# DVE order around the second projection of an attention step: one rotation ahead of a block transpose, token sums inverted ahead of both

## The chip, the cores and the metric

The kernel runs on one core of one Trainium2 chip. The metric is the device time in microseconds (us) of one execution, as the median of the runs shown. Three runs of the kernel before gave 1044.98, 1046.76 and 1047.56 us. Five engines work side by side, each on its own queue of instructions in program order, and wait for each other only through semaphores: PE (TensorE: matmuls and transposes), DVE (VectorE), ACT (ScalarE), POOL (GpSimd) and SP, which issues the DMAs here.

## The reference, cut to what matters

The input is 64 sequences of 256 rows by 192 columns. Three layers follow each other:

```
# 1: token layer: 16 tokens become 8, by attention over the tokens
q = einsum('bndt,st->bnds', xv, Wq) + bq ; kv = einsum('bndt,st->bnds', xv, Wkv) + kv_bias
attn = softmax(einsum('bnds,bndr->bnsr', q * scale, k)) ; h = q' + einsum('bnsr,bndr->bnsd', attn, v)
# 2: attention over the 128 rows of a sequence, 12 query heads, 3 key and value heads of 64, rotary embedding
q, k = apply_rope(q, cos, sin), apply_rope(k, cos, sin)      # q, k, v = layernorm(h) @ Wq, Wk, Wv
h = h + softmax(q k^T * SCALE) v @ Wo
# 3: feed-forward layer, 192 -> 768 -> 192
h = h + gelu(layernorm(h) @ W_in + b_in) @ W_out
```

## The kernel before, in words

A step p handles two sequences, a = 0 and a = 1, and the three layers are staggered: the attention of pair p runs beside the token layer of pair p + 1 and the feed-forward layer of pair p - 1. The host-side function `run` writes `step` out for p = -1, 0 and 1, puts p = 2 to 30 in a loop of 29 passes, and writes out p = 31, 32 and 33. Every engine has its own `step`; the order of its work is the order of the code, written by hand.

What belongs to the attention of one sequence, and who does it: PE projects (`qkv`, three banks of the ring of that sequence, `RING[a]`); DVE multiplies each bank by the cosine and by the sine table (`rotate`, lines L491 and L493, outputs `rot_c` and `rot_s`); POOL adds the two products of banks 0 and 1 to `q_tok` (L396, one addition for a bank, 384 columns), DVE adds those of the keys to `k_tok` (`keys_added`, L501 and L504); PE turns the six tiles of `q_tok` and the two of `k_tok` (`qk_turned`, L690), ACT copies them to `qkT` (L296), and PE multiplies them to scores (L711). DVE takes the maxima (`key_max`, L515), ACT the exponentials with their sums (`score_exp`, L302), DVE inverts the sums (`sums_inverted`, L535), POOL multiplies (`probs`, L404), and DVE turns the probabilities in blocks of 32 by 32 into `EB` (`blocks_turned`, L526, a `STREAM_TRANSPOSE` for each of three groups k = 0, 1, 2). SP then moves `EB` through DRAM to `ET` so that whole rows are turned (`blocks_moved`): groups 0 and 1 make the first piece, group 2 the second. Each piece is one write (`spill`, L231) and four reads (L237). PE multiplies `ET` with the values (`probs_v`, L728).

The token layer's softmax has ACT's exponentials `t_e` with the sums `t_sum` (L340), DVE's inverse `t_rs` (L597 before, L595 after), ACT's scaling `t_a` (L344), and PE's transposes of `t_a` (L803).

The change lies on DVE only, where the second sequence's projection comes in while the first sequence's probabilities are still to be turned. SP's queue holds, in this order: first piece written, second piece written, four reads of the first, four reads of the second, and then the store of the result. In the loop the counts that semaphores are waited for depend on p, so the queue also holds register instructions between the engine's own.

Of the kernel before, what the change touches and what calls it, by code (L numbers as in the profile page):

```python
# [82 lines left out]
def program(nc, x, w_tok, b_tok, bq_row, w_att1, w_att2, wo, w_in1, w_in2, b_in, w_out,  # L83
# [4 lines left out]
    with ExitStack() as ctx:  # L88
# [102 lines left out]
        def need(eng, s, value):  # L191

            if not isinstance(value, int) or value > 0:
                eng.wait_ge(s, value)
# [239 lines left out]
        def _(dve):  # L434
# [41 lines left out]
            def step(p, att, tok, ffn, fin):  # L476
                n = p + 1

                def rotate(a, banks):

                    if banks[0] == 0:
                        need(dve, q_out, 4 * (p - 1) + 2 * a + 2)
                    for b in banks:
                        heads = 6 if b < 2 else NKV
                        src = RING[a][:, 512 * b:512 * b + heads * HD]
                        c = slice(b * BANKW, b * BANKW + heads * HD)
                        dve.wait_ge(qkv_mm, 6 * p + 3 * a + b + 1)
                        cos_t, sin_t = (rope_qc, rope_qs) if b < 2 else (rope_c, rope_s)
                        cos = cos_t[:].rearrange("p (o d) -> p o d", o=1).broadcast_to([P, heads, HD])
                        sin = sin_t[:].rearrange("p (o t d) -> p o t d", o=1, t=2).broadcast_to([P, heads, 2, HALF])  # L490
                        nc.vector.tensor_tensor(rot_c[:, a, c].rearrange("p (h d) -> p h d", d=HD),  # L491
                                                src.rearrange("p (h d) -> p h d", d=HD), cos, ALU.mult)
                        nc.vector.tensor_tensor(rot_s[:, a, c].rearrange("p (h t d) -> p h t d", t=2, d=HALF),  # L493
                                                src.rearrange("p (h t d) -> p h t d", t=2, d=HALF)[:, :, ::-1, :],
                                                sin, ALU.mult).then_inc(rot_out, 1)

                def keys_added(a):
                    need(dve, qT_mm, 4 * (p - 1) + 2 * a + 2)
                    dve.wait_ge(rot_out, 6 * p + 3 * a + 3)
                    c = slice(DQ, DQ + 2 * HD)  # L500
                    nc.vector.tensor_tensor(k_tok[:, a, 0:2 * HD], rot_c[:, a, c], rot_s[:, a, c], ALU.add)  # L501
                    c = slice(DQ + 2 * HD, DQ + DKV)
                    kc, ks = (r[:, a, c].rearrange("p (o d) -> p o d", o=1).broadcast_to([P, 2, HD]) for r in (rot_c, rot_s))
                    nc.vector.tensor_tensor(k_tok[:, a, 2 * HD:].rearrange("p (o d) -> p o d", o=2),  # L504
                                            kc, ks, ALU.add).then_inc(k_out, 1)
# [14 lines left out]
                def blocks_turned(a, k, q):  # L520
                    g = GROUPS[k]
                    s0, heads = PIECES[g // 2]
                    h0 = REP * g - s0
                    dve.wait_ge(prob_out, 6 * q + 3 * a + k + 1)
                    need(dve, spilled[g // 2], 16 * (2 * (q - 1) + a + 1))
                    nc.vector.transpose(  # L526
                        EB[:, a, s0 * P:(s0 + heads) * P].rearrange("p (j h c) -> p h j c", j=NB, h=heads)[:, h0:h0 + REP],
                        E[:, a, 512 * g:512 * (g + 1)].rearrange("p (h j r) -> p h j r", h=REP, j=NB)
                    ).then_inc(blocks_out, 1)
# [11 lines left out]
                def attention_stats(a, done):  # L541
                    dve.wait_ge(h2_out, done)
                    stats(h2, st2, mv2, a, ln2_st, ln2_mv, done)
# [46 lines left out]
                    sums_inverted(0, 2, p)  # L590
                if ffn:
                    attention_stats(1, 2 * p)
                if att:
                    blocks_turned(0, 1, p)
                if tok:  # L595
                    dve.wait_ge(t_exp, 2 * n + 2)
                    nc.vector.reciprocal(t_rs[:], t_sum[:]).then_inc(t_rcp, 1)  # L597
                if att:
                    rotate(1, (0, 1))
                    blocks_turned(0, 2, p)  # L600
                    rotate(1, (2,))
                    keys_added(1)
# [47 lines left out]
                if att:  # L650
# [4 lines left out]
                    attention_stats(0, 2 * p + 1)  # L655

            run(dve, step)

        @block.tensor
# [280 lines left out]
```

## Time and profile before

| | |
|---|---|
| median of three runs | 1046.76 us |
| profiled execution, its own time | 1043.57 us |
| its span | 1041.7 us |
| granted TensorE clock, mean | 0.986 |
| PE busy | 988.7 us, 95% of the span |
| DVE busy | 810.2 us, 78% |
| ACT busy | 730.3 us, 70% |
| POOL busy | 434.3 us, 42% |
| mean traffic of the DMA engines | 122 GB/s |

Engine names in the views: PE is the matmul side of TensorE and PEld its weight loads, which run ahead of the matmuls; SPq is SP's queue of DMA issues; DVEq are the instructions that DVE's sequencer handles alone (register operations, waits, branches) and that aren't counted as busy. A row of a timeline begins with the start from the begin of the span and the duration, both in us; at its end stands in brackets how long the engine had been idle before it, and what ended that.

### The profile page before, as it was taken

The page shows a single profiled execution, that of the slowest core. Times are in us where ns is not written, and L with a number is a line of the kernel's source. Part 1 is how long each engine was busy: PE and PEld are TensorE (multiplying, and loading weights), DVE is VectorE, ACT ScalarE, POOL GpSimd, SP SyncE. Part 2 cuts the span into 40 slices and gives each one's busy share as a digit, 9 for nine tenths or more (in the row PEclk, how much of TensorE's full clock was granted, in tenths as well). Part 3 has the DMA queues.
Part 4 walks back from the last instruction along what each step waited for, and adds up shares of the span by engine and source line. Part 5 has one row for each costly group of instructions (what it writes and reads, how often), then busy time and mean ns, then how long its engine had stood idle before and what let it go on. Part 6 is the DMA issues. An engine that isn't in the chain of part 4 may idle for free. (4 is left out here: it accounts for less than half of the span.)

```text
span 1041.7 us, 24501 instructions
## 1 busy us (share of the span) xinstructions
PE 988.7 (95%) x7232; PEld 856.5 (82%) x7232; DVE 810.2 (78%) x2095; ACT 730.3 (70%) x2531; POOL 434.3 (42%) x583
## 2 busy tenths in 40 slices
PE   3689999999999999999999999999999999999986
PEld 2567888888988888888888888888888888888875
DVE  2678888778878878888877888887788887788861
ACT  2456776787776677677677777667867767777761
POOL 0334444444544443454444444435345444434440
PEclk8789999999999999999999999999999999999999
DMA  5134434334434434443433454443444344344331
GB/s 176 43 110 132 140 103 143 120 109 128 149 119 118 139 110 119 138 141 109 135 124 105 128 149 123 113 141 110 121 134 144 113 128 128 108 121 149 109 119 46
DMA packets 139935, 127.49 MB, mean 122 GB/s; under 512 B 30992, under 2 KB 123024, under 8 KB 139920
## 3 DMA queue, kind: packets, MB, share of 16 engines
q1 hardware_dynamic: 137632, 124.16, 39.9%
q10 hardware_dynamic: 2288, 3.15, 0.9%
q8 instruction: 7, 0.11, 0.0%
q14 instruction: 8, 0.07, 0.0%
HBM read 70.63 MB, written 56.62 MB: 122 GB/s over the span
## 5 line engine op out<-in xcount | busy, mean ns | idle before, releaser
L404 POOL TENSOR_TENSOR E<-E,e_rcp 128x512 f32<-128x512 f32 x192 | 198.4, 1040 | 282.4 <-DVE e_rcp L535 279.3
L302 ACT ACTIVATE E<-ring,m_neg 128x128 f32<-128x128 f32 x768 | 271.4, 388 | 55.5 <-DVE m_neg L515 55.4
L396 POOL TENSOR_TENSOR q_tok<-rot_c,rot_s 128x384 f32<-128x384 f32 x128 | 125.4, 1000 | 127.8 <-DVE rot_s L493 127.8
L302 ACT ACTIVATION_READ_ACCUMULATOR E<-ring,m_neg 128x1 f32 x768 | 174.8, 228 | 0.0
L515 DVE TENSOR_REDUCE m_neg<-ring 128x4 f32<-128x512 f32 x192 | 122.5, 680 | 54.1 <-PE ring L711 54.1
L296 ACT COPY qkT<-ring 128x512 f32<-128x512 f32 x128 | 71.9, 587 | 127.0 <-PE ring L690 127.0
L526 DVE STREAM_TRANSPOSE EB<-E 128x512 f32<-128x512 f32 x192 | 133.9, 698 | 17.7 <-POOL E L404 17.7
L842 PE MATMUL ring<-wo_sb,OT 128*128 128x192 f32 x768 | 141.6, 335 | 1.7 <-ACT OT L310 1.7
L698 PE MATMUL bank<-wout_sb,G 128*128 128x192 f32 x768 | 135.4, 326 | 2.9 <-ACT G L370 2.9
L842 PEld LDWEIGHTS ring<-wo_sb,OT 128*128 128x128 f32 x768 | 124.3, 191 | 5.0 <-issue 2.6
L698 PEld LDWEIGHTS bank<-wout_sb,G 128*128 128x128 f32 x768 | 125.4, 190 | 3.5 <-ACT G L370 3.4
L711 PEld LDWEIGHTS ring<-qkT 64*128 64x128 f32 x1536 | 90.7, 187 | 29.8 <-ACT qkT L296 29.8
L711 PE MATMUL ring<-qkT 64*128 64x128 f32 x1536 | 103.0, 280 | 5.0 <-ACT qkT L296 1.4
L728 PE MATMUL ring<-ET,v_tok 128*64 128x512 f32 (+1 forms) x512 | 96.8, 499 | 1.1 <-DMA ET<-spill 1.1
L491 DVE TENSOR_TENSOR rot_c<-ring,rope_qc 128x384 f32<-128x384 f32 x128 | 69.8, 545 | 14.9 <-issue 12.2
L664 PE MATMUL ring<-WH,XH 128*128 128x384 f32 x192 | 73.8, 384 | 1.5 <-DVE XL L647 1.5
L493 DVE TENSOR_TENSOR rot_s<-ring,rope_qs 128x384 f32<-128x384 f32 x128 | 69.8, 545 | 0.0
L728 PEld LDWEIGHTS ring<-ET,v_tok 128*64 128x64 f32 x512 | 31.0, 136 | 46.1 <-issue 35.7
L690 PE MATMUL ring<-ident,q_tok 128*128 128x128 f32 x384 | 60.4, 280 | 7.5 <-POOL q_tok L396 7.4
L664 PE MATMUL ring<-W2S,XL 128*128 128x384 f32 x192 | 65.2, 340 | 0.0
L664 PE MATMUL ring<-WL,XH 128*128 128x384 f32 x192 | 65.2, 340 | 0.0
L664 PE MATMUL ring<-WH,XL 128*128 128x384 f32 x192 | 65.1, 339 | 0.0
(125 smaller groups left out, 2258.6 us busy)
## 6 DMA issues: line engine op xcount, KB each, us to landing
spill<-EB SPq DMA_DIRECT2D x64, 512.0 KB, 2.7
ET<-spill SPq DMA_DIRECT2D x256, 128.0 KB, 2.8
spill<-EB SPq DMA_DIRECT2D x64, 256.0 KB, 2.1
ET<-spill SPq DMA_DIRECT2D x256, 64.0 KB, 2.3
x_sb<-in_x_dram SPq DMA_DIRECT2D x64, 192.0 KB, 2.5
out_dram<-out_sb SPq DMA_DIRECT2D x64, 96.0 KB, 2.3
x_sb<-in_x_dram SPq DMA_DIRECT2D x64, 64.0 KB, 2.3
w_raw<-in_w_att_dram ACTq DMA_DIRECT2D x2, 576.0 KB, 4.8
```

Of the source, the lines that this page charges most:

```text
L296: nc.scalar.copy(qkT[:, a, c], RING[a][:, c]).then_inc(qT_out, 1)
L302: last = nc.scalar.activation(E[:, a, s * P:(s + 1) * P], RING[a][:, s * P:(s + 1) * P], ACT.Exp, bias=m_neg[:, a, s:s + 1], accum_out=e_s ...
L396: nc.gpsimd.tensor_tensor(q_tok[:, a, c], rot_c[:, a, c], rot_s[:, a, c], ALU.add).then_inc(q_out, 1)
L404: nc.gpsimd.tensor_tensor(e, e, r, ALU.mult).then_inc(prob_out, 1)
L491: nc.vector.tensor_tensor(rot_c[:, a, c].rearrange("p (h d) -> p h d", d=HD), src.rearrange("p (h d) -> p h d", d=HD), cos, ALU.mult)
L515: nc.vector.tensor_reduce(m_neg[:, a, REP * g:REP * (g + 1)], RING[a][:, 512 * g:512 * (g + 1)].rearrange("p (h k) -> p h k", k=P), AX_X, ...
L526: nc.vector.transpose(EB[:, a, s0 * P:(s0 + heads) * P].rearrange("p (j h c) -> p h j c", j=NB, h=heads)[:, h0:h0 + REP], E[:, a, 512 * g: ...
L664: last = nc.tensor.matmul(out_ap, lhsT, rhs, start=(i == 0), stop=(i == len(terms) - 1))
L698: last = nc.tensor.matmul(B6[:, a * D:(a + 1) * D], G[:, m, a * P:(a + 1) * P], wout_sb[:, m, :], start=(m == 0), stop=(m == NM - 1))
L711: last = nc.tensor.matmul(RING[a][:, s * P:(s + 1) * P], qkT[rows, a, t * P:(t + 1) * P], qkT[rows, a, k0:k0 + P], start=True, stop=True)
L728: last = nc.tensor.matmul(RING[a][k * HD:(k + 1) * HD, 512 * b:512 * b + n_cols], v_tok[:, a, g * HD:(g + 1) * HD], src.rearrange("p i h c ...
L842: last = nc.tensor.matmul(ATT_Y, OT[:, a, t * P:(t + 1) * P], wo_sb[:, t, :], start=(t == 0), stop=(t == 5))
```

## The change

It moves two instructions of DVE in every step with attention: the inverse of the token sums (with its wait) goes ahead of the block transpose of group 1 of the first sequence, and so does the rotation of bank 0 of the second sequence. The block transpose now stands between the rotations of bank 0 and bank 1. No instruction is added or removed, and the four other engines keep their queues.

```
-                if att:
-                    blocks_turned(0, 1, p)
                 if tok:
                     dve.wait_ge(t_exp, 2 * n + 2)
                     nc.vector.reciprocal(t_rs[:], t_sum[:]).then_inc(t_rcp, 1)
                 if att:
-                    rotate(1, (0, 1))
+                    rotate(1, (0,))
+                    blocks_turned(0, 1, p)
+                    rotate(1, (1,))
                     blocks_turned(0, 2, p)
                     rotate(1, (2,))
                     keys_added(1)
```

On DVE, in the body of the loop, behind the statistics of the first layer norm input `h` (BN_STATS and BN_AGGR); the instructions named ISA and REGISTER_ALU are the sequencer's own, which work out the count to wait for:

```order
 L465 BN_STATS st<-h 128x6 [waits h2_out]
 L467 BN_AGGR mv<-st 128x2 [waits ln2_st]
-L526 STREAM_TRANSPOSE EB<-E 128x4x4x32 [waits spilled_01,prob_out]
-L596 ISA
-L597 RECIPROCAL t_rs<-t_sum 128x2 [waits t_exp]
+L594 ISA
+L595 RECIPROCAL t_rs<-t_sum 128x2 [waits t_exp]
 L194 REGISTER_ALU
 L487 REGISTER_ALU [waits q_out]
 L491 TENSOR_TENSOR rot_c<-ring,rope_qc 128x384 [waits qkv_mm]
 L493 TENSOR_TENSOR rot_s<-ring,rope_qs 128x384
+L526 STREAM_TRANSPOSE EB<-E 128x4x4x32 [waits spilled_01,prob_out]
```

The transpose has moved down past a register instruction, the inverse, two more register instructions and the rotation of bank 0; what stood directly behind the aggregate is now the inverse with its wait for ACT.

On DVE in the last step with attention, p = 31, which has no token layer and no register instructions:

```order
 L467 BN_AGGR mv<-st 128x2 [waits ln2_st]
-L526 STREAM_TRANSPOSE EB<-E 128x4x4x32 [waits spilled_01,prob_out]
-L491 TENSOR_TENSOR rot_c<-ring,rope_qc 128x384 [waits qkv_mm,q_out]
-L493 TENSOR_TENSOR rot_s<-ring,rope_qs 128x384
+L491 TENSOR_TENSOR rot_c<-ring,rope_qc 128x384 [waits qkv_mm,q_out]
+L493 TENSOR_TENSOR rot_s<-ring,rope_qs 128x384
+L526 STREAM_TRANSPOSE EB<-E 128x4x4x32 [waits spilled_01,prob_out]
```

Here only the transpose and the rotation of bank 0 have changed places.

## Rows read from the trace of the kernel before

**Rows 1.** The view by windows, one pass of the loop; busy us of each engine.

```profile
core 0: us, PE busy (x) PEld busy (x) DVE busy (x) ACT busy (x) POOL busy (x), PEclk, DMA share, GB/s
500.00:530.73 30.73, 30.43 (x228) 26.53 (x227) 25.10 (x67) 22.77 (x79) 13.56 (x18) 1.00 0.42 126
```

**Rows 2.** The view of waits, whole span: us in total, times, longest.

```profile
POOL q_tok L396 <- DVE rot_s L493: 127.8, 65, 6.5
...
PEld ring L690 <- POOL q_tok L396: 16.0, 35, 1.1
...
DVE rot_c L491 <- issue: 12.2, 29, 0.5
```

**Rows 3.** The timeline of DVE in one pass of the loop.

```profile
509.19 0.18 DVE L535 RECIPROCAL e_rcp<-e_sum 128x4 f32<-128x4 f32 x1 [0.44 <-ACT E L302]
...
509.77 0.18 DVE L467 BATCH_NORM_AGGREGATE mv<-st 128x2 f32<-128x6 f32 x1 [0.16 <-DVE st L465]
509.88 0.71 DVE L526 STREAM_TRANSPOSE EB<-E 128x512 f32<-128x512 f32 x1
510.51 0.12 DVE L597 RECIPROCAL t_rs<-t_sum 128x2 f32<-128x2 f32 x1
510.55 0.53 DVE L491 TENSOR_TENSOR rot_c<-ring,rope_qc 128x384 f32<-128x384 f32 x1
511.01 0.55 DVE L493 TENSOR_TENSOR rot_s<-ring,rope_qs 128x384 f32<-128x384 f32 x1
...
511.94 0.54 DVE L493 TENSOR_TENSOR rot_s<-ring,rope_qs 128x384 f32<-128x384 f32 x1
...
514.11 0.28 DVE L504 TENSOR_TENSOR k_tok<-rot_c,rot_s 128x128 f32<-128x128 f32 x1
```

**Rows 4.** The timeline of POOL, same pass.

```profile
510.76 0.57 POOL L388 TENSOR_TENSOR rs<-ve,half_neg 128x1 f32<-128x1 f32 x1
511.63 1.96 POOL L396 TENSOR_TENSOR q_tok<-rot_c,rot_s 128x384 f32<-128x384 f32 x2 [0.31 <-DVE rot_s L493]
```

**Rows 5.** The timeline of PE's weight loads, same pass.

```profile
513.64 0.31 PEld L690 LDWEIGHTS ring<-ident,q_tok 128*128 128x128 f32 x3 [0.41 <-POOL q_tok L396]
...
514.52 0.30 PEld L690 LDWEIGHTS ring<-ident,k_tok 128*128 128x128 f32 x2
...
515.74 1.42 PEld L711 LDWEIGHTS ring<-qkT 64*128 64x128 f32 x24 [0.36 <-ACT qkT L296]
```

**Rows 6.** The timeline of ACT, same pass.

```profile
508.87 0.29 ACT L302 ACTIVATION_READ_ACCUMULATOR E<-ring,m_neg 128x1 f32 x1
...
509.64 0.28 ACT L340 ACTIVATION_READ_ACCUMULATOR t_e<-t_s,t_neg 128x1 f32 x1
510.67 0.70 ACT L344 ACTIVATE t_a<-t_e,t_rs 128x128 f32<-128x128 f32 x2 [0.74 <-DVE t_rs L597]
```

**Rows 7.** The timeline of DVE where one pass of the loop ends.

```profile
525.84 0.18 DVE L467 BATCH_NORM_AGGREGATE mv<-st 128x2 f32<-128x6 f32 x1 [0.16 <-DVE st L465]
526.45 0.56 DVE L491 TENSOR_TENSOR rot_c<-ring,rope_qc 128x384 f32<-128x384 f32 x1 [0.43 <-issue]
```

**Rows 8.** DVE's sequencer, lines L596, L194, L487: duration ns, first and last start.

```profile
L596 DVEq FUSED_REGOPS  x1: 64/64/64, 509.9 to 509.9; - x1
```

```profile
L194 DVEq ALU_OP  x1: 40/40/40, 510.0 to 510.0; - x1
```

```profile
L487 DVEq ALU_OP  x5: 40/40/40, 510.1 to 526.7; - x5
```

**Rows 9.** The timelines of SP's queue and PE's loads; the page's DMA issues.

```profile
510.70 0.35 SPq L231 DMA_DIRECT2D spill<-EB  x1
...
513.70 3.67 SPq L237 DMA_DIRECT2D ET<-spill  x8
...
521.26 0.14 PEld L728 LDWEIGHTS ring<-ET,v_tok 128*64 128x64 f32 x2 [0.29 <-issue]
...
ET<-spill SPq DMA_DIRECT2D x256, 64.0 KB, 2.3
```

More of the change, by code:

```diff
@@ L592, in step @@
                     attention_stats(1, 2 * p)
-                if att:
-                    blocks_turned(0, 1, p)
                 if tok:
@@ L598, in step @@
                 if att:
-                    rotate(1, (0, 1))
+                    rotate(1, (0,))
+                    blocks_turned(0, 1, p)
+                    rotate(1, (1,))
                     blocks_turned(0, 2, p)
```

## The prediction, written before the run

> **What bounds the kernel now.** I read the windows first. One pass of the loop takes 30.73 us, PE is busy for 30.43 of it, DVE for 25.10 and POOL for 13.56 [rows 1]. So a pass is as long as PE's queue with the few short waits in it, and the change, which leaves PE's queue alone, can act only through one of those waits. The view of waits names the one that the moved instructions lead to: PE's weight loads stand for 16.0 us in total, 35 times, before the transposes L690, until POOL has added `q_tok`; POOL in turn waits for DVE's `rot_s` [rows 2]. The loop has 29 passes, so this is a wait of every pass.
>
> Then the timelines of one pass, engine by engine, to see which of the two banks ends that wait. DVE rotates bank 0 from 510.55, with `rot_s` from 511.01 to 511.56; `rot_s` of bank 1 ends at 511.94 + 0.54 = 512.48 [rows 3]. POOL starts its two additions at 511.63, which is 0.07 behind the first `rot_s`, and is through at 511.63 + 1.96 = 513.59 [rows 4]. PE's load for the second three tiles comes at 513.64, 0.05 later, after 0.41 idle [rows 5]. So PE waits for bank 1 of `q_tok`, not for bank 0: the load before the first three tiles shows no wait. What follows on PE, the two tiles of keys at 514.52 and the scores at 515.74, which wait for ACT's copy of the turned tiles, hangs on the same chain [rows 5].
>
> When does POOL's second addition start? The two take 1.96 together, so half of that behind 511.63, at 512.61. What it needs from DVE is there at 512.48 + 0.07 = 512.55. POOL is the later one by only 0.06 us. That is the slack of the whole path; the rest of the argument is on which side of it the change lands.
>
> **What the change does, part by part.**
>
> *The transpose goes behind the rotation of bank 0.* It occupies DVE's queue for 510.51 - 509.88 = 0.63 us [rows 3]. With the inverse directly behind the aggregate, and nothing lost between, the inverse would start at 509.88 and the rotation at 510.55 - 0.63 = 509.92. Its `rot_s` would end 0.63 earlier, at 510.93. POOL can't use all of this: its `rs` runs until 510.76 + 0.57 = 511.33 [rows 4], so its first addition could start 0.30 earlier. But bank 1 is still behind the same transpose: the sum of work in front of its `rot_s` is what it was. So 512.48 stays at best, POOL's second addition can start at 512.55 at best, and the gain on PE is at most 0.06 us a pass, 29 x 0.06 = 1.7 us. Ahead of it stands the key path too: `k_tok` is done at 514.11 + 0.28 = 514.39 and isn't moved earlier, and PE starts on it at 514.52 [rows 3, 5]; with the 0.05 of a handoff to PE that is 0.08 of room, so no larger gain could pass there either.
>
> *The inverse goes in front, with its wait for ACT.* In the row order of before it stands at 510.51, when ACT has long been done. Now it's due at 509.88. ACT's second sum of `t_e` is read out at 509.64 + 0.28 = 509.92 [rows 6]. How long such a handoff takes is seen one row above: the sum of the last score exponential ends at 508.87 + 0.29 = 509.16, and DVE's inverse starts at 509.19, 0.03 later [rows 3, 6]. So the inverse starts at 509.95, and DVE has lost 0.07 us. Behind the waiting instruction is all of DVE's queue: both rotations, both transposes, the keys. That ACT's `t_a`, now at 510.67 after 0.74 idle, comes some 0.5 us earlier [rows 6] is worth nothing: PE turns `t_a` only behind the feed-forward matmuls, and that load shows no wait.
>
> *The register instructions lose their cover.* Between the inverse and `rot_c` the loop has two register instructions of the sequencer, and the second has a wait. Before, the sequencer ran through them at 510.0 and 510.1, while the engine was still in the transpose of 0.71 us, and the row of `rot_c` at 510.55 shows no idle time [rows 3, 8]. Now the engine's only work in front of them is the inverse, which takes the queue for 0.04 us (510.51 to 510.55). They show up as idle time of DVE. How much: the register instructions on L596, L194 and L487 start at 509.9, 510.0 and 510.1, so about 0.1 apart though their own durations are 0.064 and 0.040 [rows 8]. Two of them, less the 0.04 that the inverse covers, give 0.16 us. The trace has one place where this is bare: at the end of a pass the aggregate starts at 525.84 and `rot_c` at 526.45, after 0.43 us in which DVE waited for nothing but issue, and this happens 29 times, once for each pass [rows 2, 7]. There four sequencer instructions, with a branch among them, stand between. Compared with the 0.11 from an aggregate to its follower (509.77 to 509.88), they cost 0.61 - 0.11 = 0.50, or 0.13 each, which puts two of them at 0.25. From below the bound is nothing at all, if the sequencer still gets through while aggregate and inverse run. I take 0.16, the nearer row since it is of these very instructions without a branch; the ends 0 and 0.25 go to the range.
>
> The Trainium skill speaks on both sides here, and neither figure enters the sum. "Advanced Engine Details and Errata", Sequencer Loop, says that other engine instructions can be read and queued while a control instruction executes; read broadly, the register instructions stay hidden and the change costs 0.07 instead of 0.23 a pass. "Vector Engine (DVE) Microarchitecture Reference", section 1.2, says that a semaphore wait is issued before the opcode is even read and that every DVE instruction takes the full dispatch; by that nothing behind the inverse is read before ACT is done, and both register instructions are bare. The row of the loop's end, with 0.43 us of issue, sides with the second.
>
> *Sum for a pass.* DVE from the rotation of bank 1 on is later by 0.07 + 0.16 = 0.23 us. Its `rot_s` then ends at 512.71, POOL starts on it at 512.78 instead of 512.61, and PE's load moves from 513.64 to 513.81: 0.23 - 0.06 = 0.17 us. The keys, at 514.39 + 0.23 + 0.05 = 514.67, are just in time for PE at 514.52 + 0.17 = 514.69. DVE's later work of the pass (the normalised `hn` directly behind the keys, the maxima of the scores) is late by 0.23 rather than 0.17, and PE's transposes of `hn` follow those; so for PE the pass gets longer by 0.17 to 0.23, and I take 0.20. Nothing further down gives it back, as all that PE waits for in a pass is itself started by PE's results. 29 passes give 5.8 us.
>
> *The steps outside the loop.* They have no register instructions. Step 1 pays the wait of about 0.07; steps 0 and 31 nothing that I can price above 0.1. Together 0.1 us.
>
> *The DMAs.* The first piece is complete one transpose later. It moves from 509.88 to behind `rot_s` of bank 0: 0.23 late plus two rotations of 0.46, so the write issued at 510.70 goes out at about 511.85 [rows 3, 9]. The reads, from 513.70 for 3.67 us, shift by the same 1.15: the eighth is issued by 518.5. It needs 2.3 us to land: 520.8. PE loads for the second piece at 521.26 at the earliest, and 0.2 later with the change [rows 9]. That leaves over 0.4 us, so I cost it at nothing; it is the thinnest cover in this sum. SP's write of the second piece, its store of the result and the next pass's writes wait for DVE and PE anyway.
>
> In all 5.9 us. The profiled execution took 1043.57 us (its span of 1041.7 and 1.9 around it) and would take 1049.5. It lies 3.2 us below the median of the runs, 1046.76, and I put the same difference on the median: 1052.7 us.
>
> **The rivals.**
>
> *Hidden register instructions.* DVE loses only the 0.07 of the wait, the slack of 0.06 on POOL takes nearly all, and the pass grows by 0.01 to 0.07: 0.3 to 2 us, so 1047 to 1048.8. For it: the sequencer is seen ahead of its engine by half a microsecond in rows 8 against rows 3. Against it: it can't be ahead right behind a wait that it has just sat through, and 0.43 us of bare issue in every pass. This is the case in which the kernel isn't slower; it decides if `rot_c` starts before about 510.05 on the scale of these rows.
>
> *Gain.* The full 0.06 a pass from POOL's earlier first addition, which needs a wait and a dispatch that both cost nothing: 1.7 us, 1045.1. Even this is inside what a measurement can tell. A gain beyond 3 us needs a path that I haven't seen.
>
> *Absorbed.* DVE loses 0.23 us and PE its 0.2 at the transposes, but a later wait of PE in the pass is set by something that hasn't moved. PE's idle time in a pass is 30.73 - 30.43 = 0.30 in all [rows 1], so there is little to absorb it in; most could be a half, 2.9 us, 1049.6.
>
> *Late reads.* If the read of the second piece lands in 3 us or more instead of 2.3, PE waits at L728 for up to 0.3 us more in a pass, on top of the forecast: 8.7 us more, 1061.
>
> **How the numbers follow.** A change of 0.3%, 3.1 us, is about what a measurement of this kernel can tell from none. The forecast has a chance of 0.66, with its own range from 1050 (0.11 a pass) to 1055.2 (0.07 + 0.25 - 0.03 = 0.29 a pass, 8.4 us). The hidden case has 0.17, the absorbed one 0.08, late reads 0.05, a gain 0.04. Slower by over 0.3%: 0.66 + 0.05 and a third of the absorbed case, 0.73. Faster: of the gain and of what I haven't seen, 0.05. Within: 0.22. The range that is to hold 8 in 10 reaches from the hidden case to the upper end of the register cost: 1046.7 to 1055.6.
>
> **What would show it.** In a pass of the changed kernel: the inverse directly behind the aggregate, 0.15 to 0.2 behind its start, with a small wait for ACT; `rot_c` of bank 0 with 0.1 to 0.3 us idle before it that is put down to issue, 29 times; POOL's first addition right behind its `rs` and its second with idle time before it, where it had none; PE's wait at the second L690 at about 0.6 instead of 0.41; a pass of about 30.93 us. I am wrong if `rot_c` follows the inverse within 0.05 us, if the pass stays at 30.73, or if PE's loads L728 show a wait for DMA.

## The result, and the profile after

The changed kernel takes 1051.84 us in the median (1050.87 to 1052.5) against 1045.88 us for the kernel before on the same chip (1044.98 to 1047.56). The ratio is 1.0054, with a 95% interval from 1.0041 to 1.0067: slower by 4.3 to 7.0 us. The forecast was 5.9 us.

The first look is at the length of a pass, by the starts of the token inverse on DVE, twenty passes apart, in the timeline of DVE of the changed kernel:

```profile
203.71 0.17 DVE L595 RECIPROCAL t_rs<-t_sum 128x2 f32<-128x2 f32 x1
...
822.23 0.17 DVE L595 RECIPROCAL t_rs<-t_sum 128x2 f32<-128x2 f32 x1
```

(822.23 - 203.71) / 20 = 30.93 us, against 30.73 before [rows 1]. 29 passes of 0.20 us more are 5.7 us, which is the measured difference; what the few steps outside the loop add can't be told apart.

The same stretch of DVE as in [rows 3] shows where in the pass it is lost:

```profile
512.79 0.18 DVE L467 BATCH_NORM_AGGREGATE mv<-st 128x2 f32<-128x6 f32 x1 [0.16 <-DVE st L465]
512.97 0.17 DVE L595 RECIPROCAL t_rs<-t_sum 128x2 f32<-128x2 f32 x1
513.15 0.56 DVE L491 TENSOR_TENSOR rot_c<-ring,rope_qc 128x384 f32<-128x384 f32 x1
513.63 0.55 DVE L493 TENSOR_TENSOR rot_s<-ring,rope_qs 128x384 f32<-128x384 f32 x1
514.09 0.70 DVE L526 STREAM_TRANSPOSE EB<-E 128x512 f32<-128x512 f32 x1
514.72 0.52 DVE L491 TENSOR_TENSOR rot_c<-ring,rope_qc 128x384 f32<-128x384 f32 x1
515.16 0.54 DVE L493 TENSOR_TENSOR rot_s<-ring,rope_qs 128x384 f32<-128x384 f32 x1
```

Count from the aggregate. Before, `rot_s` of bank 1, the last thing that POOL needs, started 511.94 - 509.77 = 2.17 us behind it; now it is 515.16 - 512.79 = 2.37. `rot_c` of bank 1, in front of it, started at 1.70 in the kernel before (the row below, left out between two of [rows 3]) and starts at 1.93 now: DVE has lost 0.23 us there, for the same instructions.

```profile
511.47 0.55 DVE L491 TENSOR_TENSOR rot_c<-ring,rope_qc 128x384 f32<-128x384 f32 x1
```

The inverse starts 0.18 behind the aggregate, where the transpose stood at 0.11, and `rot_c` follows the inverse after 0.18 instead of 0.04. The 0.18 in front of the inverse is the wait for ACT, whose second sum of the changed kernel's pass is read out at 512.67 + 0.27 = 512.94, 0.03 before the inverse starts:

```profile
512.67 0.27 ACT L340 ACTIVATION_READ_ACCUMULATOR t_e<-t_s,t_neg 128x1 f32 x1
```

The register instruction L594 also stands in front of the inverse, but it isn't what sets this time: in step 1, which is written out and has no such instruction, the inverse follows the aggregate after 0.18 as well (79.68 and 79.86 in DVE's timeline, with ACT's sum read out by 79.84).

POOL shows what the change gave and what it took, in its timeline of the changed kernel, to be set against [rows 4]:

```profile
513.77 0.57 POOL L388 TENSOR_TENSOR rs<-ve,half_neg 128x1 f32<-128x1 f32 x1
514.31 1.00 POOL L396 TENSOR_TENSOR q_tok<-rot_c,rot_s 128x384 f32<-128x384 f32 x1
515.78 1.00 POOL L396 TENSOR_TENSOR q_tok<-rot_c,rot_s 128x384 f32<-128x384 f32 x1 [0.47 <-DVE rot_s L493]
```

The first addition now follows `rs` directly, 0.3 us earlier than before. The second stands still for 0.47 us until the rotation behind the transpose is through. PE needs the second, and its weight loads wait for it 0.60 instead of 0.41 us [rows 5]:

```profile
516.83 0.31 PEld L690 LDWEIGHTS ring<-ident,q_tok 128*128 128x128 f32 x3 [0.60 <-POOL q_tok L396]
```

Over the whole span that wait has gone from 16.0 to 22.4 us [rows 2], which is 0.2 us a pass:

```profile
PEld ring L690 <- POOL q_tok L396: 22.4, 35, 1.2
...
PEld ring L728 <- DMA ET<-spill: 3.0, 4, 1.2
```

The second line is the thin cover of the prediction. The kernel before had nearly the same wait for the reads, so the later write of the first piece costs nothing here:

```profile
PEld ring L728 <- DMA ET<-spill: 2.5, 3, 1.4
```

In the changed kernel SP's queue issues the write 514.91 - 512.79 = 2.12 us behind the aggregate, before it was 510.70 - 509.77 = 0.93 [rows 3, 9]:

```profile
514.91 1.79 SPq L231 DMA_DIRECT2D spill<-EB  x2
```

### The profile page after: what moved, and what is told of

It is laid out like the page before. It is cut to its first block and busy times, and to the rows that moved or that the text cites. A ratio compares the mean times of both kernels' runs of the same rounds, so it can differ in the third digit from the quotient of the medians.

```text
span 1049.1 us, 24501 instructions
## 1 busy us (share of the span) xinstructions
PE 990.7 (94%) x7232; PEld 858.0 (82%) x7232; DVE 815.1 (78%) x2095; ACT 731.5 (70%) x2531; POOL 434.5 (41%) x583
## 5 line engine op out<-in xcount | busy, mean ns | idle before, releaser
L664 PE MATMUL ring<-W2S,XH 128*128 128x384 f32 x192 | 65.2, 339 | 0.0
```

Source lines behind the costliest of these rows:

```text
L664: last = nc.tensor.matmul(out_ap, lhsT, rhs, start=(i == 0), stop=(i == len(terms) - 1))
```

## The experiments

The time of a pass is, as above, from the starts of the inverse twenty passes apart; ratios are against the kernel before on the same chip. "To bank 1" is the time from the aggregate to `rot_c` of bank 1 on DVE, in a pass in the middle of the span, and good to 0.01 us, as the rows are rounded. The experiments are called e1 to e3, r2, b0 to b2 and d1, as in the table.

| kernel | to bank 1, us | pass, us | ratio (95% interval) |
|---|---|---|---|
| before | 1.70 | 30.73 | 1 |
| changed | 1.93 | 30.93 | 1.0054 (1.0041 to 1.0067) |
| e1, inverse only | 1.80 | 30.83 | 1.0029 (1.0017 to 1.0041) |
| e2, rotation only | 1.81 | 30.80 | 1.0016 (1.0005 to 1.0028) |
| e3, counts ahead | 1.82 | 30.79 | 1.0028 (1.0015 to 1.0040) |
| r2, two more counts | 2.12 | 31.12 | 1.0109 (1.0093 to 1.0124) |
| b0, plain, both banks ahead | 1.31 | 30.69 | 0.9979 (0.9970 to 0.9988) |
| b1, counts and both banks ahead | 1.08 | 30.45 | 0.9909 (0.9895 to 0.9923) |
| b2, second transpose later | 1.07 | 30.53 | 0.9934 (0.9920 to 0.9947) |
| d1, POOL's copy ahead | 1.71 | 30.87 | 1.0017 (1.0007 to 1.0026) |

**The inverse alone.**

```
+                if tok:
+                    dve.wait_ge(t_exp, 2 * n + 2)
+                    nc.vector.reciprocal(t_rs[:], t_sum[:]).then_inc(t_rcp, 1)
                 if att:
                     blocks_turned(0, 1, p)
-                if tok:
-                    dve.wait_ge(t_exp, 2 * n + 2)
-                    nc.vector.reciprocal(t_rs[:], t_sum[:]).then_inc(t_rcp, 1)
-                if att:
                     rotate(1, (0, 1))
```

> Only the inverse of the token sums goes ahead; the transpose follows it directly and both rotations stay behind the transpose, with their register instructions. Theory A (my sum: two separate losses on DVE, the wait for ACT and the uncovered register instructions): the inverse starts 0.18 behind the aggregate, the transpose about 0.08 behind that, DVE is late by 0.11 to 0.15 instead of 0.23, and less the 0.06 of POOL's slack the pass takes 30.78 to 30.82 us instead of 30.73: 1.5 to 2.6 us slower than before. Theory B (all of the loss is the inverse in front with its wait): DVE late by 0.23, pass 30.93, 5.6 us slower. Theory C (it is the transpose behind the rotation and the late first write): no loss, 0 us.

```profile
542.42 0.18 DVE L467 BATCH_NORM_AGGREGATE mv<-st 128x2 f32<-128x6 f32 x1 [0.16 <-DVE st L465]
542.59 0.17 DVE L595 RECIPROCAL t_rs<-t_sum 128x2 f32<-128x2 f32 x1
542.68 0.71 DVE L526 STREAM_TRANSPOSE EB<-E 128x512 f32<-128x512 f32 x1
543.31 0.52 DVE L491 TENSOR_TENSOR rot_c<-ring,rope_qc 128x384 f32<-128x384 f32 x1
```

In the timeline of DVE of e1 the inverse starts 0.17 behind the aggregate, and the transpose 0.09 behind the inverse. With the transpose as cover, `rot_c` follows it after 0.63, as in the kernel before. The loss is 0.10 us on DVE and 0.10 in the pass: half of the change's, so theory B (all of it is the inverse) and theory C (none of it) both fall. It is a little more than theory A's upper end in the pass (30.82) and in the kernel (3.0 us slower, 1.8 to 4.3, against 2.6), since nothing of POOL's slack of 0.06 took it up. The expectation had overlooked why: here bank 0 is late as well, so POOL's two additions start later as one piece and end 546.33 - 542.42 = 3.91 behind the aggregate, against 513.59 - 509.77 = 3.82 before [rows 3, 4].

```profile
544.37 1.96 POOL L396 TENSOR_TENSOR q_tok<-rot_c,rot_s 128x384 f32<-128x384 f32 x2 [0.41 <-DVE rot_s L493]
```

**The rotation alone.**

```
                 if att:
+                    rotate(1, (0,))
                     blocks_turned(0, 1, p)
...
                 if att:
-                    rotate(1, (0, 1))
+                    rotate(1, (1,))
```

> Only the rotation of bank 0 goes ahead of the transpose; the inverse stays behind the transpose, in front of the rotation of bank 1. Theory A: no wait for ACT, but two register instructions bare behind the aggregate: rot_c 0.20 to 0.26 behind the aggregate instead of the 0.11 of a covered follower, DVE late by 0.1 to 0.15, pass 30.77 to 30.82, 1.2 to 2.6 us slower than before. Theory B (all of it is the inverse): 0 us or up to 1.7 us faster. Theory C (late first write): the same as the change, 5.6 us slower.

```profile
542.84 0.18 DVE L467 BATCH_NORM_AGGREGATE mv<-st 128x2 f32<-128x6 f32 x1 [0.16 <-DVE st L465]
543.04 0.56 DVE L491 TENSOR_TENSOR rot_c<-ring,rope_qc 128x384 f32<-128x384 f32 x1
```

Here only the two register instructions stand between the aggregate and `rot_c`, and no wait for ACT: 0.20 us from start to start in DVE's timeline of e2, against 0.11 for the transpose in the kernel before. DVE loses 0.11 by bank 1, the pass 0.07. Theory A holds. POOL's first addition is early here, so the slack counts: the second ends 546.72 - 542.84 = 3.88 behind the aggregate, 0.06 later than before for a DVE that is 0.11 late.

```profile
545.72 1.00 POOL L396 TENSOR_TENSOR q_tok<-rot_c,rot_s 128x384 f32<-128x384 f32 x1 [0.36 <-DVE rot_s L493]
```

In this kernel the write of the first piece comes nearly as late as in the change (the transpose starts 1.14 us behind the aggregate, there 1.30), and the kernel loses a third of it, so theory C falls again.

**The counts ahead.** The order of the change, with the counts of the first rotation and its waits put between BN_STATS and BN_AGGR (in the file by a function that is handed to `stats`, for the second sequence only; shown here where it takes effect).

```
                 nc.vector.bn_stats(st[:, a, :], src[:, a, :]).then_inc(s_st, 1)
+                need(dve, q_out, 4 * (p - 1) + 4)
+                dve.wait_ge(qkv_mm, 6 * p + 4)
```

> The order of the change, but the counts and waits of the rotation of bank 0 are worked out between the two statistics instructions, where the engine waits anyway, so no register instruction stands between inverse and rotation. Theory A: inverse to rot_c 0.08 us instead of 0.18, DVE late by 0.13, pass 30.80 to 30.83, 3 us faster than the change and about 2 to 2.5 slower than before. Theory B and theory C: no difference from the change, 5.6 us slower than before.

```profile
540.92 0.18 DVE L469 BATCH_NORM_AGGREGATE mv<-st 128x2 f32<-128x6 f32 x1
541.12 0.17 DVE L602 RECIPROCAL t_rs<-t_sum 128x2 f32<-128x2 f32 x1
541.20 0.54 DVE L498 TENSOR_TENSOR rot_c<-ring,rope_qc 128x384 f32<-128x384 f32 x1
```

From inverse to `rot_c` it is now 0.08 us, where the change has 0.18: the register instructions cost 0.10 together. The pass is 0.14 shorter than that of the change. The ratio of the whole kernel is less sharp (1.0028, 1.6 to 4.2 us slower than before), but its interval ends just below where the change's begins.

**Two more of them.** Dose against effect: two further waits in front of the changed kernel's rotation, for counts long reached, which bring two more register instructions.

```
                 if att:
+                    need(dve, q_out, 4 * p - 5)
+                    need(dve, q_out, 4 * p - 3)
                     rotate(1, (0,))
```

> The changed kernel with two more register instructions of the sequencer (two further waits on the same semaphore for lower counts, long reached) between the inverse and the rotation of bank 0. Theory A (bare register instructions cost about 0.085 to 0.1 us each on DVE and nearly as much in the pass): inverse to rot_c 0.35 to 0.38 us instead of 0.18, pass 31.07 to 31.12 us instead of 30.92, 10 to 11.5 us slower than before. Theory B (they are hidden or it is the pipeline's own restart): pass 30.92, 5.7 us slower than before like the change.

```profile
547.61 0.17 DVE L595 RECIPROCAL t_rs<-t_sum 128x2 f32<-128x2 f32 x1
547.99 0.56 DVE L491 TENSOR_TENSOR rot_c<-ring,rope_qc 128x384 f32<-128x384 f32 x1 [0.21 <-PE ring L666]
```

0.38 us from inverse to `rot_c`, 0.20 more than in the change, and the pass grows by 0.19 to 31.12 us: about 0.1 us for each such instruction, on DVE and in the pass alike. The kernel is 11.4 us slower than before. The idle time has a label that misleads. The last matmul of that bank, in PE's timeline below, is through at 546.88, 1.1 us before `rot_c`; what DVE waited for was its own sequencer.

```profile
546.54 0.34 PE L666 MATMUL ring<-W2S,XL 128*128 128x384 f32 x1
```

**Both banks ahead.** The same parts as the change, with the transpose behind both rotations instead of between them.

```
                 if att:
-                    rotate(1, (0,))
-                    blocks_turned(0, 1, p)
-                    rotate(1, (1,))
+                    rotate(1, (0, 1))
+                    blocks_turned(0, 1, p)
                     blocks_turned(0, 2, p)
```

> The change with one thing different: the block transpose goes behind the rotations of both banks instead of between them; the inverse with its wait stays in front and the register instructions stay bare. Theory A: DVE loses its 0.23 us but rot_s of bank 1 is no longer behind the transpose, so POOL's second addition follows the first at once and q_tok is complete 0.25 us earlier than before, POOL's copy lets the keys through earlier, and what then sets PE is hn on DVE, about as late as before or 0.05 later: pass 30.68 to 30.78, 1.5 us faster to 1.5 slower than before, in any case 4 us or more faster than the change. Rival (the keys' own work on DVE sets PE, late by 0.23): pass 30.85 to 30.93, 3.5 to 5.8 us slower than before.

```profile
539.89 1.96 POOL L396 TENSOR_TENSOR q_tok<-rot_c,rot_s 128x384 f32<-128x384 f32 x2
541.80 0.49 POOL L418 COPY h_cur<-h_next 128x384 f32<-128x384 f32 x1
```

```profile
543.05 0.20 PEld L689 LDWEIGHTS ring<-ident,k_tok 128*128 128x128 f32 x2 [0.23 <-DVE k_tok L504]
543.57 0.42 PEld L827 LDWEIGHTS bank<-ident,hn 128*128 128x128 f32 x4 [0.32 <-DVE hn L473]
```

POOL's two additions run without a gap (first fence), and PE no longer waits for `q_tok` in the loop; it waits 0.23 us for the keys and 0.32 for `hn` instead (second fence, PE's weight loads). The kernel is 2.2 us faster than the one before (1.3 to 3.1), a little more than expected, of which 29 passes of 0.04 us are 1.3. DVE carries the same two losses as in the change. So what denied the change its gain is that the second bank stayed behind the transpose.

**Both banks and the counts ahead.** As b0, with the counts ahead as in e3, and with the inverse between the two rotations instead of in front of them.

> Counts ahead as in e3_counts_ahead; then the rotation of bank 0, the inverse, the rotation of bank 1, and only then the two transposes and the keys. Theory A: rot_c 0.10 behind the aggregate, nothing lost; POOL's first addition follows its rs at once and its second follows without idle time, so q_tok is done 0.25 to 0.3 us earlier; but the keys are where they were, with 0.08 of room, and hn with less: pass 30.65 to 30.73, 0 to 2.3 us faster than before. Theory C (late first write): the first piece is complete 1.5 us later than before, PE waits at L728 and the kernel is over 5 us slower.

```profile
535.13 0.18 DVE L469 BATCH_NORM_AGGREGATE mv<-st 128x2 f32<-128x6 f32 x1
535.23 0.52 DVE L498 TENSOR_TENSOR rot_c<-ring,rope_qc 128x384 f32<-128x384 f32 x1
...
536.13 0.15 DVE L604 RECIPROCAL t_rs<-t_sum 128x2 f32<-128x2 f32 x1
536.21 0.54 DVE L498 TENSOR_TENSOR rot_c<-ring,rope_qc 128x384 f32<-128x384 f32 x1
...
539.03 0.29 DVE L508 TENSOR_TENSOR k_tok<-rot_c,rot_s 128x128 f32<-128x128 f32 x1
539.24 0.28 DVE L511 TENSOR_TENSOR k_tok<-rot_c,rot_s 128x128 f32<-128x128 f32 x1
```

`rot_c` comes 0.10 behind the aggregate, so neither loss is left. The kernel takes 1035.40 us in the median against 1045.08, a ratio of 0.9909: 9.5 us less by the ratio, of which 29 passes of 0.28 us are 8.1. That is far more than the 2.3 us of theory A's upper end, and theory C falls. The size of the gain was the surprise, and the last two rows have a reason: the first keys addition takes 0.29 us here and the second follows after 0.21. In the change, and in the kernel before it, the first took 0.45 to 0.47 and the second followed after 0.36 to 0.40. The keys are done 539.52 - 535.13 = 4.39 us behind the aggregate, before it was 514.39 - 509.77 = 4.62 [rows 3].

**What holds the keys.** In the kernel before, POOL's copy of `h_next` to `h_cur`, which follows the second `q_tok` addition, is put ahead of POOL's `rs`.

```
+                if att:
+                    wait_apart(pool, pool_passed, (h2_out, 2 * p))
+                    nc.gpsimd.tensor_copy(h_cur[:], h_next[:]).then_inc(h_kept, 1)
                 if ffn:
                     rstd2(2 * p, 1)
                 if att:
                     turned_in(1)
-                    wait_apart(pool, pool_passed, (h2_out, 2 * p))
-                    nc.gpsimd.tensor_copy(h_cur[:], h_next[:]).then_inc(h_kept, 1)
```

> The kernel before, with POOL's copy of h (the one behind the second q_tok addition, 0.50 us) put ahead of the second layer norm's rstd. It delays POOL's rs to 511.83 on the scale of the rows before and with it q_tok by about 0.2 us. Theory D (the first keys addition on DVE, which reads two tiles of SBUF, can't finish while POOL works): with POOL idle behind q_tok the key addition L501 takes 0.29 instead of 0.47 us and the next starts 0.20 behind it instead of 0.40, the keys no longer hold PE, but q_tok does: pass 30.85 to 30.95, 3.5 to 6 us slower than before. Rival (the 0.47 is the addition's own time): L501 stays at 0.47.

```profile
548.11 0.29 DVE L502 TENSOR_TENSOR k_tok<-rot_c,rot_s 128x128 f32<-128x128 f32 x1
548.32 0.28 DVE L505 TENSOR_TENSOR k_tok<-rot_c,rot_s 128x128 f32<-128x128 f32 x1
```

```profile
546.15 1.96 POOL L396 TENSOR_TENSOR q_tok<-rot_c,rot_s 128x384 f32<-128x384 f32 x2
550.00 0.50 POOL L422 COPY h_kept<-h 128x384 f32<-128x384 f32 x1 [1.90 <-issue]
```

DVE's order is that of the kernel before; only POOL is free from 548.11 on. The addition takes 0.29 and the next starts 0.21 behind it, where the kernel before had 0.47 and 0.40. Theory D holds. The changed kernel has the held case in the same two views:

```profile
516.93 0.45 DVE L501 TENSOR_TENSOR k_tok<-rot_c,rot_s 128x128 f32<-128x128 f32 x1
517.29 0.28 DVE L504 TENSOR_TENSOR k_tok<-rot_c,rot_s 128x128 f32<-128x128 f32 x1
```

```profile
516.72 0.50 POOL L418 COPY h_cur<-h_next 128x384 f32<-128x384 f32 x1
```

The copy ends at 517.22 and the second addition starts 0.07 later. In the kernel before it is the same 0.07, from 513.54 + 0.50 = 514.04 to 514.11 [rows 3]:

```profile
513.71 0.47 DVE L501 TENSOR_TENSOR k_tok<-rot_c,rot_s 128x128 f32<-128x128 f32 x1
```

```profile
513.54 0.50 POOL L418 COPY h_cur<-h_next 128x384 f32<-128x384 f32 x1
```

So the keys on DVE hung on POOL's chain as well. It explains b0, too: there POOL's copy is over before the keys are added, and they are done 4.63 us behind the aggregate, as early as before, though DVE has lost its 0.2 us. The pass of d1 grew by 0.14, at the lower edge of what was expected, while the kernel as a whole lost 1.8 us (0.7 to 2.7) and not the 3.9 of 29 passes. The two traces don't show where the rest went: outside the 29 passes d1 takes 1047.2 - 29 x 30.87 = 152.0 us in its trace, and the kernel before 1041.7 - 29 x 30.73 = 150.5. But the profiled execution of d1 was the longest of its ten, and that of the kernel before, at 1043.57 us, one of the shortest. In both traces the granted clock is 1.00 from 80 to 1000 us and lower only at the two ends (0.66 in d1 from 50 to 60 us, 0.83 before). The whole-kernel times may carry a microsecond or two from there, so the pass is the sharper figure.

**The second transpose later still.** As b1, with the transpose of group 2 behind the keys and `hn`.

> As b1_both_banks_ahead, but the block transpose of group 2 goes behind the keys and hn. Theory A: hn is 0.6 us earlier and PE's wait for it (0.23 before L836) goes; the scores wait for ACT's copy alone; the second piece of the spill is written 1.3 us later but is the smaller one and is written before the reads of the first end, so no DMA wait: pass 30.20 to 30.30 instead of 30.45, 14 to 17 us faster than before. Rival (the DMA waits, which b1_both_banks_ahead shows 23 times already, grow): pass over 30.45, no gain over b1_both_banks_ahead.

It is 6.9 us faster than before but 2.6 slower than b1 by the ratios, a pass of 30.53 against 30.45. PE no longer waits for `hn`, yet its scores start as late: 543.49 - 537.83 = 5.66 us behind the aggregate, in b1 540.78 - 535.13 = 5.65. The rows are PE's loads for the scores, of b2 and then of b1:

```profile
543.49 1.44 PEld L719 LDWEIGHTS ring<-qkT 64*128 64x128 f32 x24 [0.48 <-ACT qkT L296]
```

```profile
540.78 1.42 PEld L719 LDWEIGHTS ring<-qkT 64*128 64x128 f32 x24 [0.27 <-ACT qkT L296]
```

The wait for `hn` in b1 lay beside the one for ACT's copy of the keys. What was later, measured from that load, is `HL` on DVE, which the feed-forward matmuls need, again b2 and then b1:

```profile
544.22 0.67 DVE L627 TENSOR_TENSOR HL<-bank,HH 128x512 fp32r<-128x512 f32 x1
```

```profile
541.40 0.69 DVE L627 TENSOR_TENSOR HL<-bank,HH 128x512 fp32r<-128x512 f32 x1 [0.17 <-ACT HH L352]
```

In b1 DVE is there 0.17 before ACT and starts 0.62 behind the scores' first load; in b2 DVE comes straight from its queue and starts 0.73 behind. The waits for the spilled reads also grew, from 10.5 us in 23 times in b1 to 17.9 us in 36 times in b2 (2.5 us in 3 times before, 9.4 in 15 in b0): with both banks ahead the late reads are no longer free. How the difference in time divides between the two isn't settled. My expectation for b2, 14 to 17 us faster than before, was twice what came of it.

## Why the prediction was right, and where it was not

*The end.* PE's queue sets the pass, and the change acts through the wait for bank 1 of `q_tok`: right. The forecast was 0.20 us a pass and 5.9 us in all; measured are 0.20 and 4.3 to 7.0. That the figure is so close is in part luck, as the next two points show.

*DVE's loss of 0.23 us.* Right to the hundredth as a sum, but one term was too small and the other too large, and the errors cancel. The wait was put at 0.07. The inverse did start 0.07 later than its place (0.18 behind the aggregate instead of 0.11), but it also occupies the queue for 0.08 to 0.09 there, instead of the 0.04 that it had behind the transpose, so e1 shows 0.10. The register instructions were put at 0.16; e3 shows 0.10 to 0.11, r2 about 0.10 for each one that is fully bare, and e2 0.11 for two of them behind an aggregate that covers some. The mistake was to let the inverse cover only 0.04 of them, when it covers its 0.08 to 0.09.

*From DVE to the pass.* The sum had 0.17 us at PE's load, and 0.17 it is: POOL's second addition ends 516.78 - 512.79 = 3.99 behind the aggregate instead of 3.82, and PE's load stands at 516.83 - 512.79 = 4.04 instead of 3.87. The step from 0.17 to 0.20 had another reason than the true one. It said that the keys and `hn` on DVE would be late by the full 0.23. But `hn` starts 517.50 - 512.79 = 4.71 behind the aggregate, before it was 514.31 - 509.77 = 4.54, so it's late by 0.17 as well; the rows are of the changed kernel and then of the kernel before:

```profile
517.50 0.37 DVE L471 TENSOR_SCALAR hn<-h,mv,rs 128x192 f32<-128x192 f32 x1
```

```profile
514.31 0.37 DVE L471 TENSOR_SCALAR hn<-h,mv,rs 128x192 f32<-128x192 f32 x1
```

The last 0.02 to 0.03 of the pass comes somewhere between that load and the next pass's aggregate; where, isn't shown.

*The hidden case.* It fell with e3 and r2. Of the two passages of the Trainium skill that the prediction set against each other, the runs side with "Vector Engine (DVE) Microarchitecture Reference", section 1.2, as far as they go: in the traces of the change, e1, r2 and b0 the next instruction of the sequencer starts 0.01 to 0.02 us behind the inverse that has waited for ACT, and never before it. The wait for ACT isn't even needed for them to be bare: e2 has none in front of them, only the aggregate, which has itself just waited for the statistics. Behind a long instruction the register instructions are hidden, as the 0.04 between inverse and `rot_c` before shows [rows 3], so the passage on the Sequencer Loop in "Advanced Engine Details and Errata" isn't contradicted either; the one holds right behind a wait, the other where the engine has long work before it.

*The absorbed case and the late reads.* Neither happened in the change. POOL's slack of 0.06 us is borne out where bank 0 goes ahead of the transpose: `q_tok` is 0.17 late for 0.23 on DVE in the change, 0.06 for 0.11 in e2, 0.06 for 0.12 in e3 and 0.36 for 0.42 in r2. In e1, where bank 0 stays behind, there is none, and 0.10 stays 0.10.

*The keys.* This part was wrong. The prediction said that the keys are done at 514.39, that they aren't moved earlier, and that no gain over some 0.08 us could pass them. That is one of the two reasons why the rival of a gain was bounded at 1.7 us; the other, that bank 1 stays behind the transpose, held. It took the 0.47 us of the first addition for its own time. b1 and d1 show that 0.2 us of it is waiting for POOL, so a faster `q_tok` lets the keys through earlier too, and b1 gained 0.28 us a pass. For the forecast of this change it made little difference, as POOL's second addition wasn't earlier here; it is the reason, though, why the keys and `hn` are late by 0.17 and not by 0.23.

*The tell.* I expected 29 rows of idle time in front of `rot_c`, put down to issue. There are none: the view of waits has 12.0 us in 28 times, before it was 12.2 in 29 [rows 2], all at the end of the pass. The record of the inverse is 0.17 us long and fills the 0.18 to the next start. The loss shows in the distance of the starts alone.

## What to carry to other kernels

An instruction that is short and has just waited covers little behind it; each register instruction that a loop needs for a semaphore's count then cost DVE about 0.1 us here, so work the counts out in front of a wait that is there anyway. Before putting work between two halves of something that another engine needs whole, ask which half it waits for: here the first half early was worth nothing, and both halves early were worth 2.2 us even with the losses, and 9.5 us without them. A duration in a profile may hold waiting: compare the same instruction where its neighbours are idle before you call it fixed.

## What the runs showed of the hardware that I had not expected

- A DVE addition that reads two tiles of SBUF (128 columns each) was stretched while POOL ran: 0.29 us with POOL idle, 0.45 to 0.47 beside its copy of 0.50 us, and the next instruction started 0.07 behind the end of the copy. In b1 the copy was nearly over when the addition began, and it took 0.29. In b2 it is the second addition that meets the copy, and it takes 0.58. The multiplications by the rope tables, which read one input from PSUM, kept their 0.52 to 0.56 us throughout. No semaphore of the code stands between the copy and the additions, so the engines don't wait for each other only through semaphores, as it says ahead of the prediction; what the two share is not shown by these runs.
- A register instruction of DVE's sequencer has a record of 0.040 us [rows 8] and costs about 0.10 where nothing covers it (r2).
- A 128x2 inverse occupies DVE's queue for 0.04 us behind a transpose, with a record of 0.12, and for 0.08 to 0.09 behind an aggregate that has waited, with a record of 0.17. It isn't only the empty engine that makes it longer: in b1 it follows a rotation without idle time, and takes 0.08 with a record of 0.15.
